# Routed experts: row transposes one unit ahead, gathers of four units ahead of the stage, and stores awaited later

## What is computed

```python
x = x + cross_attention(layernorm(x), ctx)
h = layernorm(x)                          # input of the ffn layer, own residual inside
x1 = h + causal_attention(rmsnorm(h, ln1)) @ wo
t = rmsnorm(x1, ln2).reshape(2048, 512)
probs = softmax(t @ gate_w.T)             # 16 experts, top 6 of them, normalized to 1
for e in range(16):                       # I = 352
    routed += cw[:, e] * ((silu(t @ eg_w[e].T) * (t @ eu_w[e].T)) @ ed_w[e].T)
shared = (silu(t @ sg_w.T) * (t @ su_w.T)) @ sd_w.T      # 704 wide
out = x + x1 + routed + shared
```

## Time and profile before

| | |
|---|---|
| median of 3 runs | 2272.8 us (2270.62 to 2274.03) |
| profiled execution | 2274.86 us |
| its span in the trace | 2273.0 us |
| granted TensorE clock, mean share | 0.979 |
| TensorE matmuls busy | 2154.1 us (95%) |
| TensorE weight loads busy | 1870.6 us (82%) |
| VectorE busy | 1159.6 us (51%) |
| GpSimd busy | 966.3 us (43%) |
| ScalarE busy | 710.2 us (31%) |

### The profile page before, as it was taken

The page is one execution under the profiler, slowest core; times in us unless marked ns, Lnnn a source line. Parts: engine busy times, 40 slices in busy tenths (PEclk is TensorE's granted clock), DMA queues, the critical chain, the costliest instruction groups (busy, mean ns, idle before and its releaser), DMA issues. The chain is left out here.

```text
span 2273.0 us, 39678 instructions
## 1 busy us (share of the span) xinstructions
PE 2154.1 (95%) x11914; PEld 1870.6 (82%) x11915; DVE 1159.6 (51%) x2531; ACT 710.2 (31%) x1831; POOL 966.3 (43%) x1025
## 2 busy tenths in 40 slices
PE   6879999999999999999996999979999999999997
PEld 5668888989888898888875767779999999999996
DVE  5745646464655646465666576623333333333342
ACT  5633434343433434343434111012222222222221
POOL 1225454553645454553605035424444444444443
PEclk9989999999999999999998999989999999999998
DMA  3113344343434344343416111076776676667443
GB/s 134 61 47 112 126 153 138 123 172 120 139 124 152 112 159 154 111 168 114 158 38 245 43 65 46 33 248 157 189 196 156 179 200 162 157 182 201 83 78 56
DMA packets 139827, 300.64 MB, mean 132 GB/s; under 512 B 16704, under 2 KB 16704, under 8 KB 137472
## 3 DMA queue, kind: packets, MB, share of 16 engines
q1 hardware_dynamic: 114528, 241.25, 30.1%
q0 software_dynamic: 24960, 58.21, 13.5%
q10 hardware_dynamic: 288, 0.53, 0.1%
HBM read 177.51 MB, written 122.42 MB: 132 GB/s over the span
## 5 line engine op out<-in xcount | busy, mean ns | idle before, releaser
L567 POOL TENSOR_TENSOR chunk_hi<-chunk_raw,zero 128x512 fp32r<-128x512 f32 x153 | 159.3, 1041 | 242.2 <-DMA chunk_raw<-in_whole 242.2
L1575 DVE TENSOR_TENSOR prod<-ps,silu 128x352 f32<-128x352 f32 x111 | 58.2, 525 | 313.2 <-PE ps L62 274.4
L569 POOL TENSOR_TENSOR chunk_raw<-chunk_raw,chunk_hi 128x512 fp32r<-128x512 f32 x153 | 197.7, 1292 | 12.0
L785 DVE TENSOR_TENSOR pT_lo<-ps,pT_hi 128x384 fp32r<-128x384 f32 (+2 forms) x256 | 111.1, 455 | 176.5 <-ACT pT_hi L726 172.6
L1425 POOL DMA_INDIRECT out<-y,sidx x111 | 176.6, 1591 | 55.9 <-issue 35.1
L1432 POOL TENSOR_TENSOR carry<-ident 128x1 f32<-128x1 f32 x218 | 41.1, 188 | 327.1 <-DVE gidx L1572 256.7
L757 DVE SCALAR_TENSOR_TENSOR HS<-ps,rinv,HS 128x512 f32<-128x512 f32 x260 | 176.6, 738 | 2.8 <-PE ps L62 2.8
L715 ACT ACTIVATE prob<-ps,negmax 128x512 f32<-128x512 f32 (+3 forms) x256 | 131.6, 527 | 110.0 <-DVE negmax L746 110.0
L60 PE MATMUL ps<-wv_or_qk_hi,hT_hi 128*128 128x256 f32 x512 | 146.2, 286 | 8.3 <-POOL wv_or_qk_lo L562 8.3
L60 PE MATMUL ps<-ring,xT_0hi 128*128 x448 | 150.5, 336 | 1.7 <-DMA ring<-split_weights 1.7
L60 PE MATMUL ps<-ring,hT_hi 128*128 x333 | 140.8, 423 | 10.7 <-issue 9.0
(11 more groups left out here) (298 smaller groups left out, 6100.2 us busy)
## 6 DMA issues: line engine op xcount, KB each, us to landing
ring<-split_weights SPq DMA_DIRECT2D x240, 272.0 KB
chunk_raw<-in_whole SPq DMA_DIRECT2D x153, 256.0 KB, 2.6
split_weights<-chunk_hi SPq DMA_DIRECT2D x153, 256.0 KB, 2.4
split_weights<-chunk_raw SPq DMA_DIRECT2D x153, 256.0 KB, 2.6
xg<-in_wqk SPq DMA_DIRECT2D x16, 512.0 KB, 3.6
x<-in_x SPq DMA_DIRECT2D x4, 1024.0 KB, 5.6
xg<-in_wv SPq DMA_DIRECT2D x8, 512.0 KB, 4.0
x_spill<-x SPq DMA_DIRECT2D x4, 1024.0 KB, 3.9
```

The source lines that it names most:

```text
L567: nc.gpsimd.tensor_tensor(chunk_hi[k][:], chunk_raw[k][:], zero[:].to_broadcast([P, CH]), ALU.add).then_inc(chunk_high, 1)
L569: nc.gpsimd.tensor_tensor(chunk_raw[k][:].bitcast(F32R), chunk_raw[k][:], chunk_hi[k][:].bitcast(F32), ALU.subtract).then_inc(chunk_low, 1)
L785: nc.vector.tensor_tensor(pT[1][:, 0:split, w], ps_t[k % 2][:, 0:split * P].rearrange("p (j t) -> p j t", t=P), pT[0][:, 0:split, w].bitca ...
```

## The change

- On TensorE a step now takes the row transposes of unit n+2, the register loads, `products(n)`, `gate_up(n+1)` and `down(n)`, in this order. The first two units' rows are transposed before the loop, ahead of the first register loads.
- ScalarE and VectorE copy rows out one unit earlier; on VectorE `weigh` comes before `low_rows`, and the index copy behind both.
- In `shared_expert` GpSimd gathers four units instead of two. In the routed stage, each scatter comes one step earlier beside the gathers.
- The stores into `out` are waited for in `routed_experts`: by SyncE ahead of its first load of weights, and by GpSimd ahead of its second gather. The pad of zeros is stored in `normed_again` with another such pad, and a memset of `silu` falls away.
- The memset of `prod` covers its last 32 columns only.

```diff
 def shared_expert(...):
+            sp.wait_ge(pe_u, NI * STEPS)
+            load_ring(1, slice(GU, EW))
             for i in range(ST):
                 t = TT - ST + i
                 sp.wait_ge(dve_acc, ST * (STEPS - 1) + i + 1)
-                if i == 0:
-                    sp.wait_ge(pe_u, NI * STEPS)
-                    load_ring(1, slice(GU, EW))
                 sp.dma_start(out[NB - 1][:, i, :], HS[:, t * D:(t + 1) * D]).then_inc(stored, 16)
-            sp.wait_ge(dve_z, 1)
-            for pad in pad_out:
-                sp.dma_start(pad, silu[:]).then_inc(stored, 16)
-            sp.wait_ge(stored, 16 * (NB - 1 + ST + len(pad_out)))
...
-            for q, (buf, landed) in enumerate(zip(first_rows, ld_rows)):
-                nc.gpsimd.indirect_dma_start(buf[:, 0, :], None, rows, bass.IndirectOffsetOnAxis(ap=token_of[:, q:q + 1], axis=0),
+            for u in range(EARLY_UNITS):
+                nc.gpsimd.indirect_dma_start(first_rows[u % 2][:, u // 2, :], None, rows,
...
 def routed_experts(...):
         def _(sp):
+            sp.wait_ge(stored, STORED)
...
-            def step(n, q, scatters=True, gathers=True):
+            def step(m, q, scatters=True, gathers=True):
                 if gathers:
-                    pool.wait_ge(dve_i, ONE + n + 1)
-                    pool.wait_ge(pe_x, ONE + n + 1)
-                    take_waits(2 * n)
+                    pool.wait_ge(dve_i, ONE + m - 1)
+                    pool.wait_ge(pe_x, ONE + m + 1)
+                    take_waits(2 * m - 4)
                     gather(q)
                 if scatters:
-                    pool.wait_ge(dve_y, ONE + n - 1)
-                    pool.wait_ge(added, FIRST + 16 * (n - 2))
+                    pool.wait_ge(dve_y, ONE + m - 2)
+                    pool.wait_ge(added, FIRST + 16 * (m - 3))
...
-                    scatter(q)
+                    scatter(1 - q)
...
-            nc.gpsimd.memset(prod[:], 0.0).then_inc(pool_0, 1)
+            nc.gpsimd.memset(prod[:, I:NI * P], 0.0).then_inc(pool_0, 1)
...
+            for m in range(2, 4):
+                if m == 3:
+                    pool.wait_ge(stored, STORED)
+                step(m, m % 2, scatters=m > 2)
...
-            def step(n, turn, q, before=2):
-                transposed(turn + 1 + q, 1 - q)
-                if before:
-                    previous = base(n - 1)
-                following, its_expert = base(n + 1), expert(n + 1)
-                if before:
-                    down(previous, n - 1, 1 - q, before > 1)
+            def step(n, turn, q, half=0, rows=True, following=True, weighed=True):
+                if rows:
+                    transposed(turn + 2, q, half)
+                own = base(n)
+                if following:
+                    at, its_expert = base(n + 1), expert(n + 1)
                 products(n)
-                gate_up(following, its_expert, n + 1, 1 - q)
+                if following:
+                    gate_up(at, its_expert, n + 1, 1 - q)
+                down(own, n, q, weighed)
+
+            pe.wait_ge(pool_0, 1)
+            for q in range(2):
+                transposed(EARLY_UNITS // 2, q)
+            first, its_expert = base(0), expert(0)
+            gate_up(first, its_expert, 0, 0)
             pe.wait_ge(pool_0, 2)
...
                 nc.scalar.activation(silu[:], ps_g[:, 0:I], ACT.Silu).then_inc(act_s, 1)
                 if more:
-                    high_rows(n + 1, 1 - q)
+                    high_rows(n + 2, q)
...
             def step(n, q, before=True, gathers=True, more=True):
-                if gathers:
-                    nc.vector.tensor_copy(gidx[q][:], token_of[:, bass.ds(n + 2, 1)]).then_inc(dve_i, 1)
...
                 nc.vector.tensor_tensor(prod[:, 0:I], ps_u[:, 0:I], silu[:], ALU.mult).then_inc(dve_p, 1)
-                if more:
-                    low_rows(n + 1, 1 - q)
                 if before:
                     weigh(n - 1, 1 - q)
+                if more:
+                    low_rows(n + 2, q)
+                if gathers:
+                    nc.vector.tensor_copy(gidx[q][:], token_of[:, bass.ds(n + 4, 1)]).then_inc(dve_i, 1)
```

More of the change, by code:

```diff
@@ L45 @@
 SLOTS = 3
+EARLY_UNITS = 4
 CH = 512
@@ L976, in shared_expert @@
 def shared_expert(nc, sem, ps, ident, HS, hT, logits, token_of, weight_of, expert_of, base_of, ends_of,
-                  slab, warm, ring, split_w, out, pad_out, first_rows, rows, ld_rows, ld_ring, added, begin):
+                  slab, warm, ring, split_w, out, stored, first_rows, rows, ld_rows, ld_ring, added, begin):
     NBLK = T // S
@@ L1450, in _ @@
             nc.gpsimd.memset(carry[:], 0.0).then_inc(pool_0, 1)
-            nc.gpsimd.memset(prod[:], 0.0).then_inc(pool_0, 1)
+            nc.gpsimd.memset(prod[:, I:NI * P], 0.0).then_inc(pool_0, 1)
             pool.wait_ge(pool_0, 2)
             pool.wait_ge(added, FIRST)
-            for n in range(2):
-                step(n, n, scatters=False)
-            with pool.Fori(1, TURNS) as g:
+            for m in range(2, 4):
+                if m == 3:
+                    pool.wait_ge(stored, STORED)
+                step(m, m % 2, scatters=m > 2)
+            with pool.Fori(2, TURNS + 1) as g:
                 for q in range(2):
                     step(2 * g + q, q)
-            for n in range(2 * TURNS, UNITS + 2):
-                step(n, n % 2, gathers=n + 2 < UNITS)
+            for m in range(2 * TURNS + 2, UNITS + 3):
+                step(m, m % 2, gathers=m + 2 < UNITS)
             pool.wait_ge(added, FIRST + 16 * UNITS)
@@ L1464, in _, with transposed @@
         def _(pe):
-            def transposed(n, q):
-                pe.wait_ge(ld_x[q], 16 * n)
+            def transposed(landed, q, half=0):
+                pe.wait_ge(ld_x[q], 16 * landed)
                 for j in range(DC):
-                    last = nc.tensor.transpose(ps_x[q][:, j * P:(j + 1) * P], xg[q][:, 0, j * P:(j + 1) * P], ident[:])
+                    last = nc.tensor.transpose(ps_x[q][:, j * P:(j + 1) * P], xg[q][:, half, j * P:(j + 1) * P], ident[:])
                 last.then_inc(pe_x, 1)
@@ L1502, in products @@
                 last.then_inc(pe_h, 1)
-            def step(n, turn, q, before=2):
-                transposed(turn + 1 + q, 1 - q)
-                if before:
-                    previous = base(n - 1)
-                following, its_expert = base(n + 1), expert(n + 1)
-                if before:
-                    down(previous, n - 1, 1 - q, before > 1)
-                products(n)
-                gate_up(following, its_expert, n + 1, 1 - q)
+            def step(n, turn, q, half=0, rows=True, following=True, weighed=True):
[4 more added lines that the diff above has]
+                    at, its_expert = base(n + 1), expert(n + 1)
+                products(n)
+                if following:
[6 more added lines that the diff above has]
+            gate_up(first, its_expert, 0, 0)
             pe.wait_ge(pool_0, 2)
-            first, its_expert = base(0), expert(0)
-            transposed(1, 0)
-            gate_up(first, its_expert, 0, 0)
             for n in range(2):
-                step(n, 0, n, before=n)
-            with pe.Fori(1, TURNS) as g:
+                step(n, 0, n, half=1, weighed=False)
+            with pe.Fori(1, TURNS + 1) as g:
                 for q in range(2):
                     step(2 * g + q, g, q)
[L1523 to L1528, removed]
+            for n in range(2 * TURNS + 2, UNITS):
+                step(n, n // 2, n % 2, rows=n + 2 < UNITS, following=n + 1 < UNITS)
         @block.scalar
@@ L1541, in step @@
                 if more:
-                    high_rows(n + 1, 1 - q)
+                    high_rows(n + 2, q)
                 act.wait_ge(pe_h, ONE + n + 1)
                 nc.scalar.copy(hT[0][:], ps_h[:, 0:NI * P].rearrange("p (c t) -> p c t", c=NI)).then_inc(act_h, 1)
-            act.wait_ge(pool_0, 2)
-            high_rows(0, 0)
+            for q in range(2):
+                high_rows(q, q)
             for n in range(2):
                 step(n, n)
-            with act.Fori(1, TURNS) as g:
+            with act.Fori(1, TURNS + 1) as g:
                 for q in range(2):
                     step(2 * g + q, q)
-            for n in range(2 * TURNS, UNITS):
-                step(n, n % 2, more=n + 1 < UNITS)
+            for n in range(2 * TURNS + 2, UNITS):
+                step(n, n % 2, more=n + 2 < UNITS)
         @block.vector
@@ L1582, in step @@
                                         hT[0][:].bitcast(F32), ALU.subtract).then_inc(dve_h, 1)
-            dve.wait_ge(pool_0, 2)
             dve.wait_ge(added, FIRST)
-            low_rows(0, 0)
+            for q in range(2):
+                low_rows(q, q)
             for n in range(2):
@@ L1592, in _ @@
             for n in range(2 * TURNS, UNITS):
-                step(n, n % 2, gathers=n + 2 < UNITS, more=n + 1 < UNITS)
```

(3 more changed lines are left out.)

22 lines of the change are left out of this document (11 added, 11 removed).

## The result

The changed kernel takes **2254.78 us** in the median (2254.28 to 2257.74, four runs), the kernel before 2273.41 beside it: a ratio of 0.9923, 95% interval 0.9908 to 0.9938. The prediction was 2254 [2248, 2265]. The profiled execution took 2254.28 us (span 2252.5), 20.6 less than that of before.

What follows compares the result with a forecast made beforehand. TensorE was taken as the bound, losing 17.0 us to its own sequencer in the routed loop. Loop -16.3, start -2.8 and norm stage +0.4 gave -18.7: 2256.2 us profiled, a median of 2254, range 2248 to 2265, chance 0.68.

Steps and rivals of the forecast that it cites:

- The bound and its place: Routed stage, 1521 to 2105 us: TensorE loses 17.0 us waiting for its own sequencer behind the row transposes.
- Late gathers, 13 us: Routed loop: 21 units with late rows lose some 13 us; gathers issued 10.3 us ahead remove it.
- Slow loads, a remainder of 2.3 us: Routed loop: the longer queue ahead of the register loads covers most slow ones; 2.3 of the 17 us stay.
- The path with the new wait for hT, 6.3 of 7.1 us: TensorE's sequencer, row transposes through `hT_lo`, `down` and loads: done after 6.3 us, `products` due at 7.1, 0.8 spare.
- no change: Rival, chance 0.06: that path takes 7.3 us instead of 6.3, a unit 6.86, the time about 2270.
- slower: Rival, chance 0.08: VectorE's weighing waits for scatters and delays `hT_lo`; path 7.5 us, a unit 7.06, the time 2292.
- One change of work less, -1.6: Routed loop: one group of transposes per unit instead of two saves 0.015 us in 109 units, 1.6 us.
- The start, -2.8: Routed stage's start: barrier 1.0 us later, yet gate_up(0) -1.1, gate_up(1) -1.0, fourth unit's late gather 0.7; between 0 and -6.
- The pad in the norm stage, +0.4: Before the routed stage: a 256 KB store of zeros ahead of the row stores costs 0.4 us, 0 to 0.8.
- the tail, 0: Kernel's end: nothing changes, the scatters go one after the other from the same last `down`.
- The sum: Whole kernel: loop -16.3, start -2.8, before that +0.4, together -18.7; profiled execution 2256.2, median 2254.

Runs made afterwards that it cites:

- new_order_late: The changed kernel with its order on TensorE, but each gather issued later, 7.2 us ahead of its transposes: 2268.3 us, ratio 0.9976 to the kernel before.
- after_again: The changed kernel unchanged, measured once more beside some of the variants: 2254.2 us, ratio 0.9908 to the kernel before.

## Why the prediction was right, step by step

- **The bound and its place: right.** TensorE's own sequencer lost 16.4 us behind the row transposes, and these are gone.
- **Late gathers, 13 us: the share was too large.** With only the gathers moved, the rest falls by 9.7 us. Sorted again, the kernel before has 9.7 us in 14 units without a slow load and 6.7 in 18 with one. I had counted units as late whose rows landed some 2.5 us ahead and whose loss was a slow load. The lead itself was foretold well: 10.4 us measured for 10.3.
- **Slow loads, a remainder of 2.3 us: wrong, it is 0.** The step that failed was its size, "a load that takes 0.6 longer than its 0.3 is just covered", kept as a loss to be careful. Slow loads of up to 0.97 us leave no stall in `new_order_late`, 52 units of 52, nor in the changed kernel; the one such loss above needed a late `hT_lo` besides. Only 5 of 322 loads are slow in the changed kernel, for a reason I had not seen (below). The Trainium skill (TensorE: Matmul & The Clock Gate, section "Architectural detail: the array is 16× 32×32, not 1× 128×128") gives this engine's queue a depth of 64, and by that the remainder was 0: an estimate of 2253.9 for the profiled execution, where 2254.3 was measured, and of 2252 for the median. No run here shows the 64. The loads begin 2.84 us ahead of the row transposes in the median, 2.08 before, some 18 matmuls ahead in both orders as estimated. What holds them back is a wait in both: `hT_lo` now, `low_rows` before, 0.04 us behind which the sequencer goes on.
- **The path with the new wait for hT, 6.3 of 7.1 us: right, and a little shorter.** The sequencer waits for `hT_lo` in nearly every unit, and the three loads are done 5.9 us (6.1 in units with the loop's branch) behind the start of the row transposes. The two rivals that needed 7.3 with three loads, no change and slower, fall with it. That two loads more would make it 7.8 and a unit 7.36, where 7.37 was measured, is luck: that unit is the sequencer's own work with slow loads in it. My argument against "slower", that the scatter has more time now, didn't hold on VectorE (30.8 us of waiting instead of 0.8); the spare of the path was what kept it harmless.
- **One change of work less, -1.6: wrong, it is 0.** The periods in the steady stretch are 6.68 us in the kernel before and 6.69 after. I worked with a floor of 6.667, which came from a window: a count in a window of 140 us takes in the instructions that overlap its edges, two of 840 here. The gaps from 1521 us on add up to 15.7 us, not to the 17.0 of that floor.
- **The start, -2.8: right in sign, short in size.** gate_up(0) came 1.9 us earlier, not 1.1, since the drain ended 0.1 us behind the old barrier and not 1.0: it goes by the landing of the last gather, not by its instruction. gate_up(1) came another 1.7 earlier: 1.0 as forecast, since its rows are ready, and 0.7 since the clock returned 3.4 us earlier, which the bounds had and the forecast not. The fourth unit's late gather (0.7) went too. Together some -4.3 instead of -2.8.
- **The pad in the norm stage, +0.4, and the tail, 0:** VectorE reaches the last drain of the shared stage at the same time in both profiles, so the pad costs nothing that shows. But `after_again`, the same kernel, reached it 0.5 us earlier: one pair of profiles can't tell 0.4 us.
- **The sum** was -18.7 for the profiled execution, and -20.6 was measured; the median fell by 18.6, as its two profiled executions stood 1.5 us above and 0.5 us below their medians. The single terms are off by up to 3 us, and they cancel: the median met the forecast better than the working did.

## What to carry to other kernels

A register load on a sequencer is part of a closed path: work out when it must start, how much is queued in front of the array then, and what the sequencer waits for just before. Add up the sequencer's own work per unit too: with two loads more, that and not the path set the time. Where an engine idles for its own "issue", ask first whether the wait ahead of the loads or the loads themselves are late; here it was about 10 us to 7, and each has another cure (an earlier gather, or more work queued in front of the loads). A gather issued ahead of a barrier is also a wait in it, until it has landed.

## What the runs showed of the hardware

A register load on TensorE's sequencer takes 0.30 us (0.65 with its bookkeeping), unless it starts 1.8 to 3.0 us behind the issue of a scatter with add of 128 rows of 2 KB: from 1515 us on, of 309 such loads in the twelve profiles with this scatter, 212 took over 0.4 us, up to 1.0. Of 3869 loads at any other distance one did. Ahead of any scatter the first load behind the barrier took 0.49 to 0.50 us in every kernel, unexplained. Where the loads fall against the scatters decides it: in the changed kernel 7 of 322 fell there (5 slow), in `new_order_late` 95 of 321 (67 slow). Without scatters none of 322 was slow. That the load waits while the scatter's rows are read or written is how I read it; which of these was not tried.

The drain of GpSimd at the shared stage's end took 0.3 us where no gather stood ahead of it, 0.6 right behind the landing of gathers, and otherwise lasted until 0.25 to 0.33 us behind the last gather's landing (12 profiles). At the kernel's end it took 7.1 to 9.0 us.
